# A macaron block: the prologue reordered so that the first feed-forward tile opens before all weights are examined

## The chip, the cores and the metric

One NeuronCore of a Trainium2 chip runs the whole program. The time is the device time of one execution in microseconds (us).

## The reference, cut to what matters

Input x has 8 x 1024 tokens of 256 features, all float32. Three residual steps follow each other:

```python
x = x + 0.5 * ffn(layernorm(x))      # ffn(r) = r + 0.5 * (silu(h(r) @ w1 + b1) @ w2 + b2)
x = x + mixer(layernorm(x))          # gated scan over time, 64 states, two projections
x = x + 0.5 * ffn(layernorm(x))
```

Here h(r) is a second layer norm with gamma and beta. The weights w1 (256 x 1024) and w2 (1024 x 256) come as int32 `q` with one scale for each group of 128 rows and each column: w = (q - 128) * scale. The products are made of `q - 128` alone and the scales are applied to the sums.

## The kernel before, in words

The 8192 tokens form 16 tiles of 512. Each stage (feed-forward, mixer, feed-forward) loops over the tiles; the whole input stays in SBUF (`resid`). Each engine has its own instruction list, written by hand, in which the work of neighbouring tiles is interleaved; semaphores join the lists. The slots of a feed-forward tile are f = 0 to 7, one for each block of 128 hidden features.

In slot f TensorE makes `half_products` (block f, first 128 features; two products of 128x512, for the rounded part `h_hi` and the remainder `h_lo`), one product pair `fc2` for each output half of block f - 4 (`LAG = 4`), and `add_products` (block f - 1, second 128 features). Between the two halves of fc1 the bank in PSUM is multiplied by `ratio` and gets `bias` (`scale_half`, on ScalarE, for f = 4 and 6 on VectorE). ScalarE then makes two silu (`g_full`, `g_hi`), GpSimd the remainder (`g_low`, L410), and VectorE adds each fc2 result to `z_acc` (`add_group`, L762). The layer norm of tile t + 2 (t + 1 in the prologue) is spread over the slots: `statistics` (L699) and `variance` on VectorE, `rsqrt` and most of `normalise` on GpSimd, the transposes (`turn`, L1002) on TensorE, `round_h` on ScalarE and `lower_h` (L745) on VectorE.

The kernel must also find out whether a weight is so large that its rounded form does not hold it exactly. `largest_of` reduces each quarter of `q` on VectorE as it lands (q1 in two pieces, q2 in two), `join_largest` joins the four, TensorE turns the column of maxima into a row, `find_width` reduces that and writes `wide_flag`. TensorE loads the flag (`value_load`) and branches to a program with one or with two parts for each weight. With these inputs the short one is taken.

Small vectors (scales, biases, gamma, beta and three mixer biases) are loaded as rows by 9 transfers of ScalarE's queue into `rows`, transposed once by TensorE and copied to `cols` by ScalarE. `beta_products` and `fold_beta` make the bias of fc1 out of beta, weights, scales and b1.

The order of the prologue on each engine before the change:

- ScalarE: 9 issues, silu table, `cols`, normalise blocks 2 and 3 of tile 0, `convert_q1(0)`, `round_h` twice, `convert_q1(1)`, all of q2, then the slots.
- VectorE: statistics and variance of tile 0, four `largest_of`, `join_largest`, reciprocal, `lower_h` c = 0, `find_width`, ratio, statistics and variance of tile 1, `fold_beta`, `lower_h` c = 1, a branch, then the slots; statistics and variance of tile 2 and half of tile 1's normalise in slot 3, statistics of tile 3 in slot 5, its variance in slot 7.
- GpSimd: constants, `rsqrt` of tile 0 (128x8: one column set for xhat, one for the residual), normalise blocks 0 and 1, `prepare_columns`, `residual` of tile 0, then the slots; `rsqrt` of tile 1 in slot 0.
- TensorE: transpose of rows, `turn` twice (after `cols_ready`), `beta_products(0)`, transpose of the maxima, `beta_products(1)`, branch, then slot 0 of tile 0. `turn` of tile 1 stands in slots 3 and 5.
- SyncE queue: x tile 0, q1, q2, x tiles 1 to 3, mixer weights and biases, x tiles 4 to 15.

Of the kernel before, what the change touches and what calls it, by code (L numbers as in the profile page):

```python
# [5 lines left out]
ALU = mybir.AluOpType  # L6
# [6 lines left out]
P = 128  # L13
# [8 lines left out]
def macaron_kernel(nc, x, wa, ba, wb, bb, wc, bc, wd, bd, wy, by, gamma, beta,  # L22
# [44 lines left out]
    R_AB = R_BETA + KC  # L67
    R_C = R_AB + 1
    ROWS = R_C + 1

    with ExitStack() as ctx:
# [15 lines left out]
        largest = sb("largest", [P, 6])  # L87
        wide_flag = sb("wide_flag", [1, 1], I32)
        beta_parts = sb("beta_parts", [P, KC, 2], F32R)
        beta_terms = sb("beta_terms", [P, FC, 2 * KC])  # L90
# [3 lines left out]
        ratio = sb("ratio", [P, FC])  # L94
# [9 lines left out]
        cols = sb("cols", [P, ROWS])  # L104
        ident = sb("ident", [P, P])
# [54 lines left out]
        rows_zero = sem("rows_zero")  # L160
# [9 lines left out]
        q2_ready = sem("q2_ready")  # L170
# [12 lines left out]
        wide_ready = sem("wide_ready")  # L183
# [9 lines left out]
        shift_ready = sem("shift_ready")  # L193
        xhat_ready = sem("xhat_ready")
# [96 lines left out]
        halves = (range(0, SUB // 2), range(SUB // 2, SUB))  # L291
        q2_halves = (slice(0, FC // 2), slice(FC // 2, FC))
# [21 lines left out]
        def _(sp):  # L314
# [43 lines left out]
        def _(pool):  # L358
            nc.gpsimd.memset(rows[:, :], 0.0).then_inc(rows_zero, 1)
# [9 lines left out]
            def rsqrt(ln, par, twice, shares=0):  # L369
# [11 lines left out]
                nc.gpsimd.tensor_tensor(shift[:, 0:n, :], rstd[:, 0:n, :], means, ALU.mult).then_inc(shift_ready, 1)  # L381

# [60 lines left out]
            def sum_bias():  # L443

                pool.wait_ge(mixer_loaded, 16 * 12)
# [21 lines left out]
            def feed_forward(ff0, ln0):  # L467
                def tile(t, par, before, behind):
                    ff, ln = t + ff0, t + ln0
                    residual_at, normalise_at = RESIDUAL_AT[before], NORMALISE_AT[before]  # L470
                    for f in range(FC):
                        if f >= 1:
                            g_low(ff, f - 1, par)
                        elif before:
                            g_low(ff - 1, FC - 1, 1 - par)
                        elif ff0 == 0:
                            rsqrt(ln0 + 1, 1, True)
                        if ff0 == 0 and not before and f == 1:
                            normalise(ln0 + 1, 1, 1, halves[0], True)
# [6 lines left out]
                        if behind >= 2 or ff0 == 0:  # L486
                            t2, twice = (t + 2, True) if behind >= 2 else (1 - behind, False)
                            if f == RSQRT_AT[before]:
# [32 lines left out]
        def _(act):  # L521
            act.wait_ge(rows_zero, 1)
# [8 lines left out]
            for v, r, at in ((ba, R_AB, 0), (bb, R_AB, N), (bc, R_C, N)):  # L531
                act.dma_start(rows[r:r + 1, at:at + N], v.rearrange("(a n) -> a n", a=1)).then_inc(rows_loaded, 16)
# [3 lines left out]

            act.wait_ge(rows_turned, 1)
            nc.scalar.activation(cols[:, :], ps_tr2[:, 0:ROWS], ACT.Copy).then_inc(cols_ready, 1)
            act.wait_ge(cols_ready, 1)
# [23 lines left out]
            def round_mixer(part):  # L563

                act.wait_ge(mixer_loaded, 16 * 12)
# [4 lines left out]
            def scale_half(ff, f):  # L570

                act.wait_ge(half_done, FC * ff + (f + 1))
                if type(ff) is int and ff == 0 and f == SCALED_ON_ACT[0]:
# [3 lines left out]
                                     scale=ratio[:, f:f + 1]).then_inc(scaled_on_act, 1)  # L577
# [33 lines left out]
            def feed_forward(ff0, ln0):  # L611
                def tile(t, par, before, behind):
                    ff, ln = t + ff0, t + ln0
                    for f in range(FC):
# [10 lines left out]
                        if f in TURN_OUT_AT[before]:  # L625
                            c = TURN_OUT_AT[before].index(f)
# [6 lines left out]
                        if (behind >= 2 or ff0 == 0) and f == 7:  # L633
# [3 lines left out]
                if ff0 == 0:  # L637
                    normalise(ln0, 0, 0, halves[1], xhat_half_ready)
                    convert_q1(0)
                    for c in range(KC):  # L640
                        round_h(ln0, ff0, 0, c, bank=(ps_tr, ps_tr2)[c])
                    convert_q1(1)
                    for k in range(KC):
                        act.wait_ge(q2_loaded[k], 16)
                    nc.scalar.activation(q2_sb[:, :, :], q2_int[:, :, :], ACT.Copy,
# [605 lines left out]
```

## Time and profile before

| what | value |
|---|---|
| median of 3 runs | 690.57 us (689.08 to 690.64) |
| profiled execution, its own time | 690.4 us |
| its span | 687.6 us |
| busy: TensorE, ScalarE, VectorE, GpSimd | 97%, 95%, 92%, 88% |
| mean granted TensorE clock | 0.999 |
| first product of 128x512 starts | 16.94 us |

The span runs from the first to the last instruction; the execution's own time is 2.8 us longer. All windows below are in us from the start of the span. The time of an instruction in a row includes its latency, so instructions of one engine that follow each other without a gap are closer together than their durations say.

### The profile page before, as it was taken

What the parts mean: (1) busy time and instruction counts of PE and PEld (TensorE: products, weight loads), DVE (VectorE), ACT (ScalarE), POOL (GpSimd) and SP (SyncE); (2) the same over time, 40 slices, a digit from 0 to 9 for tenths busy, and PEclk for the clock granted to TensorE, in tenths of its full rate; (3) what the DMA queues carried; (4) which work ended last, traced back from release to release, by engine and by line L of the source; (5) the groups of instructions that cost most, each with busy time, mean ns of one, the idle gap of its engine ahead of it and who ended that gap; (6) DMA issues with size and microseconds to landing.
All of it is one profiled execution on the core that took longest, in us unless ns stands there. A gap on an engine that the chain in (4) does not pass through costs nothing.

```text
span 687.6 us, 13669 instructions
## 1 busy us (share of the span) xinstructions
PE 668.0 (97%) x3224; PEld 539.2 (78%) x3224; DVE 634.8 (92%) x1329; ACT 653.4 (95%) x1095; POOL 604.8 (88%) x673
## 2 busy tenths in 40 slices
PE   3999999999999999999999999999999999999997
PEld 3678888888888878778877887788888888888885
DVE  5789999999999999889999998899999999999987
ACT  4899999999999999889999999999999999999994
POOL 4899999999999999857766789999999999999973
PEclk9999999999999999999999999999999999999999
DMA  8670000000000000000000000000000000000001
GB/s 254 172 236 4 1 0 0 0 0 0 0 0 0 1 0 2 1 1 1 0 0 0 0 1 1 30 33 32 31 31 31 31 31 31 31 31 32 32 32 63
DMA packets 19962, 20.22 MB, mean 29 GB/s; under 512 B 1564, under 2 KB 19666, under 8 KB 19922
## 3 DMA queue, kind: packets, MB, share of 16 engines
q1 hardware_dynamic: 19824, 19.74, 9.3%
q8 instruction: 16, 0.26, 0.2%
q14 instruction: 24, 0.20, 0.1%
q10 hardware_dynamic: 98, 0.02, 0.0%
HBM read 11.37 MB, written 8.39 MB: 29 GB/s over the span
## 4 chain that ended last, share of the span: by engine, by line
PE 90%; ACT 3%; DVE 3%; issue 2%; DMA 1%; ACTq 0%; POOL 0%; DVEq 0%; POOLq 0%
PE ps_z L1009 38%; PE ps_fc L1009 33%; PE ps_fc L1142 8%; PE ps_tr L1002 5%; PE ps_tr L1070 4%; PE ps_fc L1150 2%; PE ps_z L1002 1%; DMA rows<-in_L_attn_bc 1%; DVE z_acc L762 1%; ACT ps_fc L576 1%; ACT g_hi L593 1%; DVE stats L699 1%; ACT g_full L591 0%; DVE resid L887 0%; ACTq L530 0%
## 5 line engine op out<-in xcount | busy, mean ns | idle before, releaser
L410 POOL TENSOR_TENSOR g_lo<-g_full,g_hi 128x512 fp32r<-128x512 f32 x256 | 332.9, 1300 | 24.7 <-ACT g_hi L593 21.8
L762 DVE SCALAR_TENSOR_TENSOR z_acc<-ps_z,cols,z_acc 128x512 f32<-128x512 f32 (+1 forms) x449 | 322.2, 742 | 24.2 <-PE ps_z L1009 16.4
L1009 PE MATMUL ps_fc<-h_hi,q_sb 128*128 128x512 f32 x512 | 213.4, 417 | 1.4 <-ACT ps_fc L576 1.4
L1009 PE MATMUL ps_z<-g_hi,q_sb 128*128 128x512 f32 x512 | 202.4, 395 | 0.1
L1009 PE MATMUL ps_fc<-h_lo,q_sb 128*128 128x512 f32 x512 | 202.3, 395 | 0.0
L1009 PE MATMUL ps_z<-g_lo,q_sb 128*128 128x512 f32 x512 | 200.6, 392 | 0.0
L591 ACT ACTIVATE g_full<-ps_fc,safe_scale 128x512 f32<-128x512 f32 x256 | 194.8, 761 | 3.9 <-PE ps_fc L1009 2.2
L593 ACT ACTIVATE g_hi<-ps_fc,safe_scale 128x512 fp32r<-128x512 f32 x256 | 196.2, 766 | 0.0
L576 ACT ACTIVATE ps_fc<-ps_fc,bias,ratio 128x512 f32<-128x512 f32 x193 | 157.9, 819 | 1.8 <-DVE bias L873 1.8
L1009 PEld LDWEIGHTS ps_z<-g_hi,q_sb 128*128 128x128 f32 x512 | 96.1, 188 | 25.0 <-DVE z_acc L762 2.7
L1009 PEld LDWEIGHTS ps_fc<-h_hi,q_sb 128*128 128x128 f32 x512 | 97.3, 190 | 21.0 <-ACT ps_fc L576 2.1
L1009 PEld LDWEIGHTS ps_z<-g_lo,q_sb 128*128 128x128 f32 x512 | 96.1, 188 | 20.7
L1009 PEld LDWEIGHTS ps_fc<-h_lo,q_sb 128*128 128x128 f32 x512 | 97.6, 191 | 15.8
L375 POOL TENSOR_TENSOR rstd<-var_terms,minus_half 128x8 f32<-128x8 f32 (+1 forms) x48 | 70.7, 1472 | 11.7 <-DVE neg_mean L721 7.8
L400 POOL TENSOR_SCALAR resid<-resid,res_scale,shift 128x256 f32<-128x256 f32 x128 | 72.8, 570 | 0.2
L699 DVE BATCH_NORM_STATS2 stats<-resid 128x6 f32 (+1 forms) x192 | 69.2, 409 | 2.2 <-DMA resid<-in_L_attn_x 1.8
L583 ACT ACTIVATE z_acc<-ps_z,cols 128x512 f32<-128x512 f32 x64 | 58.0, 906 | 0.1
L389 POOL TENSOR_SCALAR xhat<-resid,rstd,shift 128x256 f32<-128x256 f32 x96 | 55.5, 579 | 0.2
L1142 PE MATMUL ps_fc<-wd_sb,q_int 128*128 128x256 f32 x240 | 54.6, 379 | 0.0
L739 DVE TENSOR_SCALAR ps_fc<-ps_fc,ratio,bias 128x512 f32<-128x512 f32 x63 | 50.9, 807 | 3.5 <-PE ps_fc L1009 3.5
L559 ACT ACTIVATE xhat<-resid,shift,rstd 128x256 f32 (+1 forms) x92 | 51.0, 602 | 0.0
L1002 PE MATMUL ps_tr<-ident,xhat 128*128 128x128 f32 x320 | 48.4, 274 | 2.1 <-ACT xhat L559 1.5
(110 smaller groups left out, 820.4 us busy)
## 6 DMA issues: line engine op xcount, KB each, us to landing
resid<-in_L_attn_x SPq DMA_DIRECT2D x15, 512.0 KB, 4.6
out_x<-resid SPq DMA_DIRECT2D x15, 512.0 KB, 2.9
q_int<-in_L_ffn_fc_q SPq DMA_DIRECT2D x4, 512.0 KB, 7.3
resid<-in_L_attn_x SPq DMA_DIRECT2D x2, 256.0 KB, 3.0
out_x<-resid SPq DMA_DIRECT2D x2, 256.0 KB, 2.7
wd_sb<-in_L_attn_Wd SPq DMA_DIRECT2D x1, 256.0 KB
wy_raw<-in_L_attn_Wy SPq DMA_DIRECT2D x2, 64.0 KB
bias_rows<-in_L_attn_by SPq DMA_DIRECT2D x1, 128.0 KB
```

Source lines behind the costliest of these rows:

```text
L375: nc.gpsimd.tensor_tensor(rstd[:, 0:n, :], var_terms[:, par, 0:n, :], minus_half[:, 0:n, :], ALU.pow).then_inc(rstd_ready, 1)
L400: last = nc.gpsimd.tensor_scalar(resid[:, t, a, :], resid[:, t, a, :], res_scale[:, a:a + 1], shift[:, 1, a:a + 1], ALU.mult, ALU.add)
L410: nc.gpsimd.tensor_tensor(g_lo[:, g % 4, :], g_full[:, g % 4, :], g_hi[:, g % 4, :].bitcast(F32), ALU.subtract).then_inc(g_ready, 1)
L576: nc.scalar.activation(bank, bank, ACT.Identity, bias=bias[:, f:f + 1], scale=ratio[:, f:f + 1]).then_inc(scaled_on_act, 1)
L583: nc.scalar.activation(z_acc[:, par, n, :], bank_of(0, n, par), ACT.Identity, bias=col(R_B2 + n), scale=col(R_S2 + n)).then_inc(z_begun[n], 1)
L591: nc.scalar.activation(g_full[:, g % 4, :], bank, ACT.Silu, scale=scale)
L593: nc.scalar.activation(g_hi[:, g % 4, :], bank, ACT.Silu, scale=scale).then_inc(g_hi_ready, 1)
L699: last = nc.vector.bn_stats(stats[:, a, :], resid[:, t, a, :])
L762: nc.vector.scalar_tensor_tensor(out=z, in0=bank_of(g, n, par)[:, tokens], scalar=col(R_S2 + KC * g + n), in1=z, op0=ALU.mult, op1=ALU.add ...
L1002: last = nc.tensor.transpose(bank[:, a * P:(a + 1) * P], xhat[:, par, a, c * P:(c + 1) * P], ident[:, :])
L1009: last = nc.tensor.matmul(out, w, v, start=start and i == 0, stop=stop and i == len(pairs) - 1, skip_group_check=not start)
L1142: nc.tensor.matmul(mix_bank(t, par, half)[:, a * D:(a + 1) * D], xn[:, par, k, at:at + P], wd_sb[:, k, :], start=False, stop=False, skip_g ...
```

## The change: what it does

1. **Small vectors.** The three mixer biases leave `rows` and go straight into a new tile `mixer_cols` by three transfers of SyncE's queue (64 elements each, one to a partition) ahead of the two `bias_rows` transfers. The memset of `rows` and ScalarE's wait for it go; ScalarE issues 6 transfers instead of 9.
2. **Tile 0's layer norm.** GpSimd makes only the xhat columns first (`rsqrt_first`, 128x4), and those of the residual (`rsqrt_rest`) after `prepare_columns`. ScalarE normalises before it copies `cols`. TensorE's `turn` no longer waits for `cols_ready`.
3. **q2.** ScalarE converts the first half, GpSimd the second, after tile 0's residual.
4. **Two flags.** The maxima of q1 alone give a first flag; those of q2 are taken after `fold_beta` and `lower_h` and give a second. TensorE opens tile 0 behind the first (`opening`: slots 0 to 3, with the second transpose of maxima inside it), then waits for the second flag and branches to the program, which begins tile 0 at slot 4.
5. **fold_beta.** `ratio` now also covers the second group of scales and `beta_terms` holds b1 times the reciprocal, so two of the five steps fall away.
6. **Tile 0's slots.** Tile 1's statistics stand behind the maxima of q2; its `rsqrt` moves to slot 2 of GpSimd, its normalise blocks 0 to 3 to slot 4 of VectorE, its `turn` to slots 5 and 7, `lower_h` to 6 and 7. Statistics of tile 2 go to slot 5 and its variance to 6; statistics and variance of tile 3 both to slot 7. ScalarE's share of tile 2's normalise moves from slot 7 of tile 0 to slot 0 of tile 1.

The core of the diff:

```diff
+        FIRST_TURN_AT, FIRST_LOWER_AT = (5, 7), (6, 7)
+        FIRST_RESIDUAL_AT = {5: (0, 1), 6: (2, 3)}
+        FIRST_NORMALISE_AT, FIRST_RSQRT_AT = {7: (0, 1, 2)}, 6
...
+            for v, at, i in ((ba, 0, 0), (bb, N, 0), (bc, N, 1)):
+                sp.dma_start(mixer_cols[at:at + N, i:i + 1], v.rearrange("(n a) -> n a", a=1)).then_inc(mixer_loaded, 16)
...
+            def rsqrt_first():
+
+                pool.wait_ge(terms_ready, 1)
+                nc.gpsimd.tensor_tensor(rstd[:, 0, :], var_terms[:, 0, 0, :], minus_half[:, 0, :],
+                                        ALU.pow).then_inc(rstd_ready, 1)
+                pool.wait_ge(rstd_ready, 1)
+                nc.gpsimd.tensor_tensor(shift[:, 0, :], rstd[:, 0, :], neg_mean[:, 0, :],
+                                        ALU.mult).then_inc(shift_ready, 1)
...
-                        elif ff0 == 0:
-                            rsqrt(ln0 + 1, 1, True)
-                        if ff0 == 0 and not before and f == 1:
-                            normalise(ln0 + 1, 1, 1, halves[0], True)
+                        if ff0 == 0 and not before and f == 2:
+                            rsqrt(ln0 + 1, 1, True, 1)
...
-                    rsqrt(ln0, 0, True)
+                    rsqrt_first()
                     normalise(ln0, 0, 0, halves[0], True)
                     prepare_columns()
+                    rsqrt_rest()
                     residual(ln0, 0, 1)
+                    pool.wait_ge(q2_loaded[1], 16)
+                    nc.gpsimd.tensor_scalar(q2_sb[:, q2_halves[1], :], q2_int[:, q2_halves[1], :], -ZERO_POINT, None,
+                                            ALU.add).then_inc(q2_ready[1], 1)
...
-                        if not before and f == 3:
+                        if ff0 == 0 and not before and f == LAG:
+                            normalise(ln0 + 1, 1, 1, halves[0], xhat_ready)
+                            normalise(ln0 + 1, 1, 1, halves[1])
+                        if ff0 == 0 and not before and f == 5:
+                            dve.wait_ge(x_loaded[0], 32)
+                            dve.wait_ge(aggr_done, ln0 + 2)
+                            statistics(2)
...
+                    join_largest(0, KC)
+                    prepare_ratios()
                     lower_h(ln0, ff0, 0, 0)
+                    find_width(0, KC + 2)
                     dve.wait_ge(beta_done, KC)
                     fold_beta(1)
                     lower_h(ln0, ff0, 0, 1, ps_tr2)
+                    for k, part in enumerate(q2_halves):
+                        largest_of(KC + k, q2_int[:, part, :].rearrange("p g d -> p (g d)"), q2_loaded[k])
+                    join_largest(1, 2 * KC + 2)
+                    dve.wait_ge(x_loaded[1], 16)
+                    dve.wait_ge(aggr_done, 1)
+                    statistics(1, halves[0])
+                    find_width(1, 2 * KC + 4)
+                    statistics(1, halves[1])
+                    variance(ln0 + 1, 1)
                     prepare_wide()
...
+            def opening(narrow):
+
+                for f in range(LAG):
+                    half_products(0, 0, f, 0)
+                    if narrow and f == LAG - 1:
+                        turn_all_largest()
+                    if f >= 1:
+                        add_products(0, 0, f - 1, 0)
+
+            def turn_all_largest():
+
+                pe.wait_ge(largest_found, 2 * KC + 3)
+                turn_largest(1)
...
-            pe.wait_ge(cols_ready, 1)
             for c in range(KC):
                 turn(0, 0, c, (ps_tr, ps_tr2)[c], 2, 1)
```

## Rows read from the trace of the kernel before

**Rows 1.** Page: the chain that ended last, shares by engine

```profile
PE 90%; ACT 3%; DVE 3%; issue 2%; DMA 1%; ACTq 0%; POOL 0%; DVEq 0%; POOLq 0%
```

**Rows 2.** Timeline of TensorE: start, duration, engine, line, out<-in, count, idle before

```profile
9.72 0.31 PE L994 MATMUL ps_z<-ident,rows 48*128 48x48 f32 x1 [9.72 <-DMA rows<-in_L_attn_bc]
11.55 1.09 PE L1002 MATMUL ps_tr<-ident,xhat 128*128 128x128 f32 x4 [1.52 <-ACT xhat L559]
...
13.14 1.85 PE L1055 MATMUL ps_z<-beta_parts,q_sb 128*128 128x2 f32 x8
...
15.21 1.87 PE L1055 MATMUL ps_z<-beta_parts,q_sb 128*128 128x2 f32 x8
16.94 0.77 PE L1009 MATMUL ps_fc<-h_hi,q_sb 128*128 128x512 f32 x1
...
19.64 0.76 PE L1009 MATMUL ps_fc<-h_hi,q_sb 128*128 128x512 f32 x1 [0.64 <-ACT ps_fc L576]
...
23.19 0.63 PE L1009 MATMUL ps_fc<-h_hi,q_sb 128*128 128x512 f32 x1
23.61 0.63 PE L1009 MATMUL ps_fc<-h_lo,q_sb 128*128 128x512 f32 x1
...
25.55 0.39 PE L1009 MATMUL ps_fc<-h_lo,q_sb 128*128 128x512 f32 x1
25.78 0.39 PE L1009 MATMUL ps_z<-g_hi,q_sb 128*128 128x512 f32 x1
...
36.88 0.50 PE L1009 MATMUL ps_z<-g_hi,q_sb 128*128 128x512 f32 x1
...
41.72 0.39 PE L1009 MATMUL ps_fc<-h_hi,q_sb 128*128 128x512 f32 x1
```

**Rows 3.** Timeline of VectorE

```profile
7.81 2.47 DVE L893 TENSOR_REDUCE largest<-q_int 128x1 f32<-128x1024 int32 x2 [1.93 <-DMA q_int<-in_L_ffn_fc_q]
...
15.26 0.28 DVE L905 TENSOR_REDUCE largest<-ps_z 1x1 f32<-1x128 f32 x1 [1.04 <-PE ps_z L1209]
...
19.72 1.41 DVE L699 BATCH_NORM_STATS2 stats<-resid 128x6 f32<-128x256 f32 x4 [0.41 <-issue]
...
21.80 0.73 DVE L729 TENSOR_SCALAR xhat<-resid,rstd,shift 128x256 f32<-128x256 f32 x2
25.98 0.82 DVE L739 TENSOR_SCALAR ps_fc<-ps_fc,ratio,bias 128x512 f32<-128x512 f32 x1 [3.46 <-PE ps_fc L1009]
...
33.20 0.73 DVE L745 SCALAR_TENSOR_TENSOR h_lo<-ps_tr,cols,h_hi 128x512 fp32r<-128x512 f32 x1
...
36.09 3.38 DVE L762 SCALAR_TENSOR_TENSOR z_acc<-ps_z,cols,z_acc 128x512 f32<-128x512 f32 x5
```

**Rows 4.** Timeline of ScalarE; ACTq is its sequencer issuing a transfer

```profile
3.94 0.27 ACTq L532 DMA_DIRECT2D rows<-in_L_attn_bc  x1
...
10.31 1.09 ACT L559 ACTIVATE xhat<-resid,shift,rstd 128x256 f32<-128x256 f32 x2
...
18.74 1.42 ACT L576 ACTIVATE ps_fc<-ps_fc,bias,ratio 128x512 f32<-128x512 f32 x2 [1.78 <-DVE bias L873]
```

**Rows 5.** Timeline of GpSimd

```profile
5.96 1.66 POOL L375 TENSOR_TENSOR rstd<-var_terms,minus_half 128x8 f32<-128x8 f32 x1 [3.62 <-DVE neg_mean L721]
...
22.21 1.47 POOL L410 TENSOR_TENSOR g_lo<-g_full,g_hi 128x512 fp32r<-128x512 f32 x1 [2.14 <-ACT g_hi L593]
```

**Rows 6.** Groups of GpSimd by form, whole span: busy us, mean ns | idle before

```profile
L410 POOL TENSOR_TENSOR g_lo<-g_full,g_hi 128x512 fp32r<-128x512 f32 x256 | 332.9, 1300 | 24.7 <-ACT g_hi L593 21.8 <-PE ps_z L1009 2.4
...
L400 POOL TENSOR_SCALAR resid<-resid,res_scale,shift 128x256 f32<-128x256 f32 x128 | 72.8, 570 | 0.2
...
L375 POOL TENSOR_TENSOR rstd<-var_terms,minus_half 128x4 f32<-128x4 f32 x16 | 17.6, 1097 | 3.6 <-POOL cs_parts L463 3.6
```

**Rows 7.** Timeline of SyncE's queue

```profile
19.27 0.56 SPq L335 DMA_DIRECT2D bias_raw<-in_L_attn_bd  x1
...
21.27 27.11 SPq L344 DMA_DIRECT2D resid<-in_L_attn_x  x12
```

More of the change, by code:

```diff
@@ L169, in macaron_kernel @@
         q1_ready = sem("q1_ready")
-        q2_ready = sem("q2_ready")
+        q2_ready = [sem(f"q2_ready{k}") for k in range(KC)]
         beta_ready = sem("beta_ready")
@@ L291, in macaron_kernel, with first_or @@
         halves = (range(0, SUB // 2), range(SUB // 2, SUB))
+        FIRST_TURN_AT, FIRST_LOWER_AT = (5, 7), (6, 7)
+        FIRST_RESIDUAL_AT = {5: (0, 1), 6: (2, 3)}
+        FIRST_NORMALISE_AT, FIRST_RSQRT_AT = {7: (0, 1, 2)}, 6
+        def first_or(ff0, before, first, usual):
+            return first if ff0 == 0 and not before else usual[before]
         q2_halves = (slice(0, FC // 2), slice(FC // 2, FC))
@@ L632, in tile @@
                             first_sum(ff, par, 1)
-                        if (behind >= 2 or ff0 == 0) and f == 7:
+                        if ff0 == 0 and before == 1 and f == 0:
+                            normalise(ln + 1, t + 1, 1 - par, REST, xhat_half_ready)
+                        if (behind >= 2 or ff0 == 0) and (ff0 or before) and f == 7:
                             normalise(ln + 2, t + 2 if behind >= 2 else 1 - behind, par, REST, xhat_half_ready)
@@ L787, in tile @@
                             add_group(ff if here else ff - 1, (f - LAG) % FC, par if here else 1 - par)
-                        if behind and f in H_LOWER_AT[before]:
-                            lower_h(ln + 1, ff + 1, 1 - par, H_LOWER_AT[before].index(f))
+                        lower_at = first_or(ff0, before, FIRST_LOWER_AT, H_LOWER_AT)
+                        if behind and f in lower_at:
+                            lower_h(ln + 1, ff + 1, 1 - par, lower_at.index(f))
                         if ff0 and not before and f == 0:
@@ L911, in prepare_wide, with lower_weights @@
+            def lower_weights(low, high, whole, full, count, ready):
+                nc.vector.tensor_scalar(whole.bitcast(F32), whole, -ZERO_POINT, None, ALU.add).then_inc(full, 1)
+                dve.wait_ge(full, count)
+                nc.vector.tensor_tensor(low, whole.bitcast(F32), high.bitcast(F32), ALU.subtract).then_inc(ready, 1)
             def prepare_wide():
-                dve.wait_ge(flag_ready, 1)
-                wide = dve.value_load(wide_flag[0:1, 0:1], min_val=0, max_val=1)
+                dve.wait_ge(flag_ready, 2)
+                wide = dve.value_load(wide_flag[0:1, 1:2], min_val=0, max_val=1)
@@ L1076, in tile @@
                     ff, ln = t + ff0, t + ln0
-                    for f in range(FC):
+                    for f in range(0 if before or ff0 else LAG, FC):
                         half_products(ff, ln, f, par)
@@ L1097, in tile @@
                             y_products(NT - 1, 1)
-                        if (behind or ff0 == 0) and f in TURN_AT[before]:
-                            c = TURN_AT[before].index(f)
+                        turn_at = first_or(ff0, before, FIRST_TURN_AT, TURN_AT)
+                        if (behind or ff0 == 0) and f in turn_at:
+                            c = turn_at.index(f)
                             if c and before:
@@ L1212, in _ @@
             pe.wait_ge(flag_ready, 1)
-            wide = pe.value_load(wide_flag[0:1, 0:1], min_val=0, max_val=1)
+            q1_wide = pe.value_load(wide_flag[0:1, 0:1], min_val=0, max_val=1)
+            with pe.If(q1_wide < 1):
+                q1_parts = (q1_sb,)
+                opening(True)
+            with pe.Else():
+                q1_parts = (q1_sb, q1_low)
+                turn_all_largest()
+                pe.wait_ge(q1_low_ready, KC)
+                pe.wait_ge(bias_ready, 1)
+                for k in range(KC):
+                    last = beta_products(k, q1_low)
+                last.then_inc(beta_low_done, 1)
+                pe.wait_ge(wide_bias_ready, 1)
+                opening(False)
+            pe.wait_ge(flag_ready, 2)
+            wide = pe.value_load(wide_flag[0:1, 1:2], min_val=0, max_val=1)
             with pe.If(wide < 1):
@@ L1218, in _ @@
                 q1_parts, q2_parts = (q1_sb, q1_low), (q2_sb, q2_low)
-                pe.wait_ge(wide_ready, KC + 1)
-                pe.wait_ge(bias_ready, 1)
-                for k in range(KC):
-                    last = beta_products(k, q1_low)
-                last.then_inc(beta_low_done, 1)
-                pe.wait_ge(wide_bias_ready, 1)
+                pe.wait_ge(q1_low_ready, KC)
+                pe.wait_ge(q2_low_ready, 1)
                 program()
```

176 lines of the change are left out of this document (86 added, 90 removed).

## The prediction

> **What bounds the kernel now.** I first read the chain of work that ended last: TensorE holds 90% of it [rows 1]. So nearly all of the span is TensorE's own work, and a prologue can only give back what lies ahead of TensorE's first unbroken stretch. Then I read TensorE's timeline. Nothing runs on it before the small vectors have landed at 9.72; `turn` of tile 0 starts at 11.55, the first product of fc1 at 16.94, then it waits 0.64 for the bias and runs on from 19.64 [rows 2]. In the first stretch the 512-column products stand 0.42 apart (23.19 to 23.61), from 25.55 on 0.23 apart: the lower and the upper level of its clock, 1.2 and 2.4 GHz [rows 2]. Slot 4 of tile 0 comes at about 25.2, slot 4 of tile 1 at 41.72 [rows 2]. The second date is my yardstick: from there on the order is the same in both kernels, each engine only waits for the others, and whatever is won or lost at 41.72 stays to the end.
>
> The timelines of the other engines say what these dates hang on. ScalarE normalises tile 0 only at 10.31, after `cols` [rows 4]. ScalarE's first scaling waits until 18.74 for the bias, which VectorE makes late because tile 1's statistics stand ahead of it [rows 4]. After its branch VectorE has a hole of 3.46 before 25.98 [rows 3]: it has made the statistics of tile 2 in front of it, at 19.72.
>
> **The change part by part: up to the first products.** Small vectors: three transfers fewer, so the last issue starts about 1.2 before 3.94 [rows 4] (three issues of some 0.3 and the wait for the memset). If the landing keeps its distance to the issue (9.7 - 3.9 = 5.7), it is at 8.5; if it goes by the count (9.7 x 6/9), at 6.5; if it is only the traffic of q1 and q2, still at 9.6. I take 7.5. What hides it is xhat: everything before 8.1 costs nothing.
>
> xhat of tile 0: the power on 128x8 took 1.66 from 5.96 [rows 5], on 128x4 it takes 1.10 [rows 6], and the 0.2 for `res_scale` falls away: shift ready at 7.3. ScalarE's two blocks (1.09, [rows 4]) end at 8.4, GpSimd's two as well. From the start of `turn` to the first product of fc1 TensorE needed 16.94 - 11.55 = 5.39, back to back [rows 2]; the same work now starts at 8.44 and ends at 13.8. Its inputs are there: `cols` follows on ScalarE at 8.4, q1's first conversion right behind it, as before; the q1 maxima are done at 10.3 (2.47 for the two from 7.81, [rows 3]). The branch on the first flag lies behind queued products, as before: nothing; if that cover is missing it costs its own length.
>
> The bias needs the last `beta_products` (13.8) and three small steps, 0.45: 14.4. The first half product is done at 13.8 + 0.85 + 0.2 = 14.9, one scaling takes 0.76 (1.42 for two, [rows 4]): the first `add_products` stands at 15.7 instead of 19.64. **TensorE's lead here: 3.9 us.**
>
> **From there to the yardstick.** Four pairs at 0.85 follow, then the transpose of all maxima at 19.1. VectorE has been ready for it: `lower_h` to 15.1, two maxima of q2 at 1.22 (2.47 for two, [rows 3]), the join, two blocks of statistics, 18.4. So it waits until 19.5, then `find_width` 0.4 (0.28 for its reduction, [rows 3]), two blocks of statistics 0.8, variance 0.7: 21.4. GpSimd's `rsqrt` of tile 1 (1.66 and two steps of 0.2, [rows 5]) ends at 23.5. In the kernel before it ended at about 20, since VectorE's normalise could start at 21.80 [rows 3]. TensorE is 3.9 early and tile 1's xhat 2 late.
>
> TensorE reaches slot 4 at 20.3. The second flag is there at 19.9. The branch is hidden: `turn` in slot 5 has to wait for xhat (24.9) anyway, some 0.9; a jump above about 1.5 us would count in full beyond that.
>
> Now VectorE has no hole left. Its list from 23.5 (each at its distance to the next: 0.66 for a 128x512 add, 3.38 for five, and for `lower_h`, 0.33 for a block of statistics, 0.70 for a scaling and for two blocks of normalise, [rows 3]): four blocks of normalise 1.40; two adds 1.32; statistics of tile 2 1.32; scaling 0.70; two adds 1.32; `lower_h` 0.66; variance 0.67; two adds 1.32; `lower_h` 0.66; statistics of tile 3 1.44; variance 0.67; the first add of group 4 0.75. Sum 12.2: it is done at 35.7. That add releases the bank for the second half of fc2's group 5, which before started at 36.88 [rows 2]. TensorE alone would have been there far earlier: 32 pairs at 0.456 and three `turn` of 0.36 are 15.7 from slot 4 to slot 4, so 36.0 at the yardstick, 4 us before VectorE lets it. **So most of the lead is spent on waiting: some 0.9 in slot 5, 0.9 in slot 7 for `lower_h`, 1.9 at about 33.8.**
>
> From 35.7 to slot 4 of tile 1 it is nine pairs and one `turn`, 9 x 0.456 + 0.36 = 4.46: 40.2, against 41.72. The same stretch took 4.84 before, 0.38 more than the sum [rows 2], for short waits on GpSimd; with those it is 40.6. The gain is 1.2 to 1.5; I take 1.2, since a sum of clean durations leaves such waits out everywhere.
>
> **What costs nothing and why.** q2's second half on GpSimd: no row has it; two inputs of 512 take 1.30, one of 256 takes 0.57 [rows 6], so 128x1024 lies between 2.0 (four times 0.5) and 2.6. GpSimd is free from 13.3 (residual of tile 0) to its first `g_low` at 17.9, and TensorE needs the half at slot 0 of tile 1; only above 4.5 would it delay anything. The three transfers of single elements on SyncE's queue: an issue took 0.56, so x tile 4 is asked for at 23 instead of 21.27 [rows 7]; it is read in tile 2, behind 41.72, and takes some 5 us. Without that cover it would be 1.7. Tile 3's x is issued ahead of them. ScalarE's normalise block in slot 0 of tile 1 is the same 0.5 as before in slot 7; GpSimd needs it only for tile 2's residual.
>
> VectorE and GpSimd side by side: the `g_low` that ran beside two blocks of VectorE's normalise took 1.47 [rows 5], the mean is 1.30 [rows 6]. Four blocks now stand beside `g_low` of groups 2 and 3: 0.3 on GpSimd, which TensorE doesn't see, as it waits for xhat there. The Trainium skill (GPSIMD Engine Reference, section Specifications) says that the two share their SBUF interfaces and get in each other's way when VectorE works in a two-port mode or with two SBUF inputs. The trace agrees by that row; if VectorE paid as well, the sum would be 0.3 worse.
>
> **The clock.** Before, the products went to the short spacing 5.6 us after the stretch from 19.64 began, in spite of products since 16.94 [rows 2]. Now the stretch begins at 15.7, so the rise is due near 21.3. Earlier gains little (VectorE binds); if it stayed at 25.2, slots 4 and 5 would take 6.8 instead of 3.7 and about 1.0 of the gain would go. The Trainium skill (TensorE: Matmul & The Clock Gate, Part 1) has the low clock as the resting state, which activity releases; the trace agrees, and it too puts the rise ahead of 25.2 here.
>
> **The rivals.** *The lead is kept.* If VectorE's list is shorter than I add it up, the 3.9 us stay: 690.4 - 3.9 = 686.5, or half of it, 688.4; [rows 1] and [rows 3] weigh against each other here. For it: TensorE is 90% of the chain. Against: VectorE was idle for 3.46 there before, and this is what the list fills. *Small vectors land as late as before* (9.6): `turn` at 9.9, everything 1.4 later, 690.6. For it: the DMA queues are full at that time. *The clock falls back* in the holes that the change makes (ends slower): TensorE stands still for 0.9, 0.9 and 1.9 us in 24 to 36. If the 1.9 drops it to the lower level, it takes another 5.6 us to rise: 13 products at 0.42 instead of 0.23, 2.6 us; 691.8. If it drops twice, 694.4; it is a slowdown that can be measured from 16 such products on. For it: with a gap of 0.64 before 19.64 the low level went on for 5 us. Against: that was before the rise, and the holes are short. *No effect*: chain unchanged is excluded, but all gains may be swallowed (jump of 3 us at the second flag): 690.6.
>
> **How the numbers follow.** The forecast: 0.60, 690.4 - 1.2 = 689.2 for an execution like the profiled one; the median of the runs is 0.17 above it, so 689.4. Lead kept wholly or by half: 0.15. Late landing or a long jump: 0.17. Clock: 0.08. About 0.3% (2.1 us) is what a measurement of this kernel can tell from no change. Faster by more: the lead kept, and a tail of the forecast, 0.18. Slower by more: half of the clock case and what I don't see, 0.07. Within: 0.75. The range: from 687.9 (two thirds of the lead kept) to 691.2 (late landing, 690.6 + 0.17, and a short wait more) leaves out about 0.2.
>
> **What would show it.** In the profile after: first `turn` at 8.4 to 8.8; first `add_products` near 15.7; spacing 0.23 from about 21; VectorE busy without a hole from 23.5 to 39; TensorE idle some 3.7 us between 20 and 36, released by VectorE; slot 4 of tile 1 at about 40.6; the rest of the span shifted as a whole. The prediction is wrong if TensorE has no idle time there, if the 0.42 spacing comes back after 25, or if later stages differ in length.

## The result: 698.8 us, 1.2% slower

| | median | runs | profiled execution, its span |
|---|---|---|---|
| before | 690.11 us | 689.08 to 690.64 | 690.4, 687.6 us |
| after | 698.76 us | 697.24 to 699.04 | 699.04, 697.2 us |

Each kernel ran four times beside the other, which is why the median of before differs a little from the one given further up. The ratio is 1.0122, with an interval of 1.0107 to 1.0137. The forecast was 689.4 with a range to 691.2 and a chance of 0.07 for slower: it was wrong in sign and by 9 us.

The page of the kernel after: span, busy time, and the shares of the chain that ended last.

```profile
span 697.2 us, 13683 instructions
...
PE 675.2 (97%) x3225; PEld 541.8 (78%) x3225; DVE 637.7 (91%) x1334; ACT 653.3 (94%) x1095; POOL 609.6 (87%) x673
...
PE 92%; DVE 3%; ACT 2%; issue 1%; POOL 1%; DMA 0%; DVEq 0%; ACTq 0%
```

The busy times of the kernel before, from its page:

```profile
PE 668.0 (97%) x3224; PEld 539.2 (78%) x3224; DVE 634.8 (92%) x1329; ACT 653.4 (95%) x1095; POOL 604.8 (88%) x673
```

TensorE is still the bound, and it has 7.2 us more busy time in a longer span. A lead or a delay of the prologue can't do that; something has made its work itself longer. The timeline of TensorE after (columns as in [rows 2]), from the first transpose to behind the yardstick:

```profile
7.33 0.31 PE L1037 MATMUL ps_fc<-ident,rows 46*128 46x46 f32 x1 [7.33 <-DMA rows<-in_L_ffn_ln_beta]
8.53 1.10 PE L1045 MATMUL ps_tr<-ident,xhat 128*128 128x128 f32 x4 [0.89 <-POOL xhat L418]
...
13.91 0.77 PE L1052 MATMUL ps_fc<-h_hi,q_sb 128*128 128x512 f32 x1 [0.20 <-issue]
...
16.04 0.77 PE L1052 MATMUL ps_fc<-h_hi,q_sb 128*128 128x512 f32 x1
...
18.66 0.39 PE L1052 MATMUL ps_fc<-h_hi,q_sb 128*128 128x512 f32 x1
...
28.39 0.77 PE L1045 MATMUL ps_tr<-ident,xhat 128*128 128x128 f32 x4 [3.63 <-DVE xhat L759]
28.80 0.78 PE L1052 MATMUL ps_fc<-h_hi,q_sb 128*128 128x512 f32 x1
...
31.08 0.63 PE L1052 MATMUL ps_fc<-h_lo,q_sb 128*128 128x512 f32 x1
31.51 0.63 PE L1052 MATMUL ps_z<-g_hi,q_sb 128*128 128x512 f32 x1
...
32.30 0.39 PE L1052 MATMUL ps_fc<-h_hi,q_sb 128*128 128x512 f32 x1
32.53 0.40 PE L1052 MATMUL ps_fc<-h_lo,q_sb 128*128 128x512 f32 x1
...
39.65 0.50 PE L1052 MATMUL ps_z<-g_hi,q_sb 128*128 128x512 f32 x1 [1.62 <-DVE z_acc L792]
...
44.41 0.39 PE L1052 MATMUL ps_fc<-h_hi,q_sb 128*128 128x512 f32 x1
```

Up to 16.04 the dates are the forecast's: `turn` at 8.53 (8.44), the first product at 13.91 (13.8), the first `add_products` at 16.04 (15.7) instead of 19.64 [rows 2]. Then TensorE stands still for 3.63 us, released by VectorE's xhat, and from there until 32.30 the products are 0.43 apart (31.08 to 31.51), the lower level of its clock. Slot 4 of tile 1, the yardstick, begins at 44.41, not at the forecast 40.6 nor at 41.72 as before. VectorE and GpSimd at that place:

```profile
19.44 0.28 DVE L945 TENSOR_REDUCE largest<-ps_z 1x1 f32<-1x128 f32 x1 [1.42 <-PE ps_z L1261]
...
21.00 0.74 DVE L745 TENSOR_SCALAR var_terms<-mean_var 128x4 f32<-128x4 f32 x1
...
24.12 4.21 DVE L759 TENSOR_SCALAR xhat<-resid,rstd,shift 128x256 f32<-128x256 f32 x4 [0.66 <-POOL shift L391]
28.25 1.40 DVE L792 SCALAR_TENSOR_TENSOR z_acc<-ps_z,cols,z_acc 128x512 f32<-128x512 f32 x2
```

```profile
13.41 2.79 POOL L530 TENSOR_SCALAR q_sb<-q_int 128x1024 fp32r<-128x1024 int32 x1
...
21.97 1.67 POOL L385 TENSOR_TENSOR rstd<-var_terms,minus_half 128x8 f32<-128x8 f32 x1 [0.24 <-DVE neg_mean L751]
...
24.05 3.81 POOL L439 TENSOR_TENSOR g_lo<-g_full,g_hi 128x512 fp32r<-128x512 f32 x3
```

The four blocks of `normalise` take 4.21 us on VectorE, where [rows 3] give 0.73 for two. They lie almost wholly beside three `g_low` of GpSimd, which take 3.81 us, 1.27 each, no more than elsewhere. GpSimd goes on undisturbed and VectorE pays: that is the first loss.

The second one is in the long stretches behind. The count of TensorE's products and transposes between 60 and 240 us, before and then after (windows; columns: busy us and count of PE, PEld, DVE, ACT, POOL, granted clock, DMA share, GB/s):

```profile
60.00:240.00 180.00, 180.00 (x878) 148.19 (x878) 173.82 (x352) 179.34 (x297) 174.41 (x198) 1.00 0.00 0
```

```profile
60.00:240.00 180.00, 180.00 (x865) 146.48 (x864) 170.64 (x347) 176.58 (x293) 172.46 (x195) 1.00 0.00 0
```

In both the engine is busy all the time and the granted clock is 1.00, yet after it gets through 13 fewer. All other engines do less as well: they follow. From 450 to 680 us it is 1101 instead of 1114; from 240 to 450 us, where the mixer lies, it is 1019 and 1020, so only the feed-forward stages lose. The timeline shows it product by product; before, then after, each from the start of an unbroken stretch to its end:

```profile
99.68 0.39 PE L1009 MATMUL ps_fc<-h_hi,q_sb 128*128 128x512 f32 x1
...
103.99 0.39 PE L1009 MATMUL ps_z<-g_lo,q_sb 128*128 128x512 f32 x1
```

```profile
101.59 0.40 PE L1052 MATMUL ps_fc<-h_lo,q_sb 128*128 128x512 f32 x1
...
104.16 0.39 PE L1052 MATMUL ps_fc<-h_hi,q_sb 128*128 128x512 f32 x1
```

Before, 19 steps in 4.31 us, 0.227 each; after, 11 steps in 2.57 us, 0.234 each, with the same duration of 0.39 in every row. From the start of one product to that of the next the mean is 0.2289 before and 0.2333 after, between 60 and 240 us; a tile of the feed-forward lasts 16.43 and 16.67 us. Over the some 30 tiles behind the yardstick that is 7.2 us, and the spans differ by 6.9 us beyond it (9.6 less the 2.7 at the yardstick); the tiles next to the mixer lose less than the others.

What can have changed there? Not the instructions. But the change resizes small tiles that are allocated ahead of the large ones (`largest`, `beta_terms`, `ratio`, `cols`, the new `mixer_cols`), and so every tile from `xhat` on (`h_hi`, `h_lo`, `g_hi`, `g_lo`, `z_acc`) lies 96 bytes further in each partition. The weights `q1_sb` and `q2_sb` are allocated ahead of them and stay. Before, h, g and the weights are all multiples of 256 bytes from each other; after, h and g are 96 bytes off. That became the main suspect.

### The profile page after: what moved, and what is told of

Same layout as the page of the kernel before. It is cut to its first block, busy times and chain, and to the rows that moved or that the text cites. A ratio compares the mean times of both kernels' runs of the same rounds, so it can differ in the third digit from the quotient of the medians.

```text
span 697.2 us, 13683 instructions
## 1 busy us (share of the span) xinstructions
PE 675.2 (97%) x3225; PEld 541.8 (78%) x3225; DVE 637.7 (91%) x1334; ACT 653.3 (94%) x1095; POOL 609.6 (87%) x673
## 4 chain that ended last, share of the span: by engine, by line
PE 92%; DVE 3%; ACT 2%; issue 1%; POOL 1%; DMA 0%; DVEq 0%; ACTq 0%
PE ps_z L1052 39%; PE ps_fc L1052 34%; PE ps_fc L1186 7%; PE ps_tr L1045 5%; PE ps_tr L1113 4%; PE ps_fc L1194 2%; PE ps_z L1045 1%; DVE stats L729 1%; DVE z_acc L792 1%; PE ps_z L1098 0%; DVE xhat L759 0%; DMA resid<-in_L_attn_x 0%; DVE resid L927 0%; DVE h_lo L775 0%; POOL h_lo L481 0%
## 5 line engine op out<-in xcount | busy, mean ns | idle before, releaser
L1052 PE MATMUL ps_z<-g_lo,q_sb 128*128 128x512 f32 x512 | 202.8, 396 | 0.0
L385 POOL TENSOR_TENSOR rstd<-var_terms,minus_half 128x8 f32<-128x8 f32 (+1 forms) x47 | 69.0, 1468 | 4.1 <-POOL cs_parts L492 3.9
L1045 PEld LDWEIGHTS ps_tr<-ident,xhat 128*128 128x128 f32 x320 | 40.0, 141 | 15.5 <-DVE xhat L759 4.1
```

The costliest lines, as they stand in the source:

```text
L385: nc.gpsimd.tensor_tensor(rstd[:, 0:n, :], var_terms[:, par, 0:n, :], minus_half[:, 0:n, :], ALU.pow).then_inc(rstd_ready, 1)
L1045: last = nc.tensor.transpose(bank[:, a * P:(a + 1) * P], xhat[:, par, a, c * P:(c + 1) * P], ident[:, :])
L1052: last = nc.tensor.matmul(out, w, v, start=start and i == 0, stop=stop and i == len(pairs) - 1, skip_group_check=not start)
```

## The experiments

All pads are tiles that nothing uses; [P, 8] is 32 bytes in each partition.

| run | what | h, g against the weights, mod 256 | us | ratio to before, interval |
|---|---|---|---|---|
| after | | 96 | 698.76 | 1.0122 (1.0107 to 1.0137) |
| e1 | after, pad 32 | 128 | 698.23 | 1.0127 (1.011 to 1.0144) |
| e2 | before, pad 32 | 32 | 695.57 | 1.0090 (1.0073 to 1.0107) |
| e3 | after, GpSimd waits | 96 | 696.73 | 1.0111 (1.0092 to 1.013) |
| e4 | e1 and e3 | 128 | 696.73 | 1.0113 (1.0096 to 1.013) |
| e5 | after, pad 416 | 0 | 692.72 | 1.0050 (1.0033 to 1.0067) |
| e6 | before, pad 512 | 0 | 689.91 | 1.0007 (0.9997 to 1.0016) |
| e7 | before, pad 128 | 128 | 695.12 | 1.0080 (1.0063 to 1.0097) |
| e8 | e5 and e3 | 0 | 690.42 | 1.0007 (0.9997 to 1.0016) |
| e9 | before, pad 256 | 0 | 689.67 | 0.9999 (0.9989 to 1.0008) |
| e10 | before, h alone by 128 | h 128, g 0 | 693.58 | 1.0048 (1.0032 to 1.0065) |
| e11 | before, g alone by 128 | h 0, g 128 | 693.37 | 1.0050 (1.0033 to 1.0066) |
| e12 | e5, layer norm earlier | 0 | 691.09 | 1.0017 (1.0007 to 1.0026) |
| e13 | before, all by 128 | 0 | 689.38 | 0.9999 (0.9989 to 1.0009) |
| e14 | before, weights alone by 128 | 128 | 695.91 | 1.0091 (1.0074 to 1.0107) |
| e15 | e8, statistics spread | 0 | 687.65 | 0.9977 (0.9968 to 0.9986) |
| e16 | e8, spread further | 0 | 690.23 | 1.0011 (1.0002 to 1.002) |

### The place of the tiles (e1, e2, e5, e6, e7, e9)

Each is one line ahead of `xhat`; of e2:

```diff
+        pad = sb("pad", [P, 8])
         xhat = sb("xhat", [P, 2, SUB, D])
```

> The changed kernel with one unused tile of 32 bytes a partition in front of xhat, so that xhat and every large tile behind it (h_hi, h_lo, g_full, g_hi, g_lo, z_acc) start at a multiple of 64 bytes again, as in the kernel before; in the changed kernel they start 32 bytes behind one. Nothing else differs. Theory A (the address sets the distance between products: 0.2333 us everywhere in the changed kernel, 0.228 in the mean before): feed-forward tiles last 16.43 us instead of 16.67, 30 tiles give back about 7 us, 698.8 becomes about 692. Rival B (the order of the prologue leaves the engines in another rhythm, addresses don't matter): within 0.5 us of 698.8. The four normalise blocks on VectorE (4.2 us) tell a third thing apart: if they are slow because xhat is no longer aligned they take 1.4 here, if it is GpSimd's work beside them they stay at 4.2.

> The kernel before with one unused tile of 32 bytes a partition in front of xhat: all large tiles from xhat on start 32 bytes behind a multiple of 64. Theory A: the products stand 0.2333 apart throughout, tiles of 16.67 us, about 690.1 + 7 = 697. Rival B: 690.1 within noise.

> The changed kernel with an unused tile of 416 bytes a partition in front of xhat. In the kernel before xhat and every large tile behind it start 128 bytes behind a multiple of 512, like resid and the weights; the run with 32 bytes only brought them to 256 behind one and gave back almost nothing. Theory A2: the distance of the products hangs on the place of the large tiles within 512 bytes (or on their distance to the weights), and 416 bytes bring back the one of before: feed-forward tiles of 16.43 us, about 698.8 - 6.5 = 692. Rival B2: the small tiles in front (ident, cols, ratio, bias), which moved too and stay moved here, or another difference of the program keep the products 0.2333 apart: 697 to 699.

> The kernel before with an unused tile of 512 bytes a partition in front of xhat: every large tile moves, but its place within 512 bytes stays. Theory A2: no change, 689.5 within noise. Rival: any move of these tiles, or only a distance beyond 512 bytes, makes the spacing 0.2333: 695 to 696, as the 32 bytes did.

> The kernel before with 128 bytes in front of xhat: all large tiles start at 256 behind a multiple of 512, as in the changed kernel with the 32-byte tile. If only the place within 64 bytes counts: 689.5. If the place within 512 counts (theory A2): 695 to 696.

> The kernel before with 256 bytes in front of xhat: the large tiles start at 384 behind a multiple of 512, thus at the same place within 256 bytes as before and at another within 512. If the place within 256 decides: 689.5. If it is the place within 512: 694 to 696.

32 unused bytes make the kernel before 6.0 us slower (e2), 128 make it 5.5 slower (e7), 256 and 512 change nothing (e9, e6). 416 on top of the change's own 96, which is 512 together, take 6.0 us off the kernel after (e5). So the place counts, and of the distances tried only multiples of 256 are free. e1 brought next to nothing: that missed its target, since 128 off is as bad as 96.

### Which tiles, and against what (e10, e11, e13, e14)

e10 moves `h_hi` and `h_lo`, e11 `g_hi` and `g_lo`, with a second pad that brings the rest back to a multiple of 512. e13 moves everything:

```diff
+        pad = sb("pad", [P, 32])
         resid = sb("resid", [P, NT, SUB, D])
```

e14 moves the weights, and what follows by 512 in all:

```diff
+        pad = sb("pad", [P, 32])
         q1_sb = sb("q1_sb", [P, KC, F], F32R)
...
+        pad2 = sb("pad2", [P, 96])
         xhat = sb("xhat", [P, 2, SUB, D])
```

> The kernel before in which only h_hi and h_lo are moved by 128 bytes within 512 (128 bytes in front of h_hi, 384 behind h_lo). If the place of the moving operand (the right-hand side that TensorE streams) makes the product slow: the products into ps_fc at 0.2333, those into ps_z as before, about half of the 5.5 us, 692. If it is the engines that write or read these tiles, or other tiles: 689.5.

> The kernel before in which only g_hi and g_lo are moved by 128 bytes within 512. By the theory of the moving operand: the products into ps_z slow, about 692. Otherwise 689.5.

> The kernel before with 128 unused bytes per partition in front of all tiles: resid, the weights, xhat, h, g and z_acc all move by 128 bytes, so their places against each other stay as they were. Theory 'relative' (what counts is where the tiles stand against each other, in pieces of 256 bytes): the time stays at 690, products 0.228 apart. Theory 'absolute' (128 behind a multiple of 256 is a good place, 0 a bad one): 695 or more, products 0.2333 apart.

> The kernel before with 128 unused bytes in front of the weights and 384 in front of xhat: the weights move by 128 bytes, xhat, h, g and z_acc by 512, which the earlier runs showed to cost nothing. Theory 'relative': as when h and g moved by 128 against the weights, 695. Theory 'absolute, of the streamed tiles': 690. Theory 'absolute, of all tiles': between, 691 to 693, since the weights alone would stand badly.

The same windows of e10, e13 and e14, a fence each:

```profile
60.00:240.00 180.00, 180.00 (x869) 147.17 (x868) 171.18 (x345) 177.56 (x295) 173.19 (x197) 1.00 0.00 0
```

```profile
60.00:240.00 180.00, 180.00 (x876) 148.04 (x876) 173.46 (x347) 178.92 (x298) 173.52 (x198) 1.00 0.00 0
```

```profile
60.00:240.00 180.00, 180.00 (x867) 146.81 (x866) 170.69 (x348) 176.63 (x294) 172.74 (x196) 1.00 0.00 0
```

All tiles moved together cost nothing (e13, 876 against 878), the weights moved alone cost 5.9 us (e14, 867) though h and g moved by 512, which alone costs nothing (e6). So it is the place of the streamed tile against the weights that counts, not the place by itself. The small tiles behind the weights moved with them in e14, but in e5 they stay where the change had put them, and the count there is 879. One of h and g moved costs 4.0 or 3.8 us (e10, e11), both 5.5 (e7): by the medians more than half each.

The loss is not spread evenly. With both operands 128 off (e7, e14), the mean step behind a product of `h_hi` or `g_hi` is 0.237 and behind one of `h_lo` or `g_lo` 0.2295, as before; at 96 off (the kernel after) all four are 0.233. In e10 it is 0.2328 behind `h_hi` and 0.2295 behind `g_hi`, but 0.2340 behind `g_lo`, which had not moved; in e11 `h_lo` is the slow one of the unmoved, 0.2339. Both stand just ahead of a product of the operand that moved. In the kernel before, a load of weights runs from 100.36 to 100.55 beside a product that streams from 100.13 to 100.52, and so with every product, so it is plausible that the two reads meet in SBUF by their distance. That is argued, not shown: in e10 neither the `g_lo` that streams nor the weights loaded beside it had moved, and that step is slow all the same. Why stays open.

### VectorE beside GpSimd (e3, e4, e8)

```diff
+                        if ff0 == 0 and not before and f == 3:
+                            pool.wait_ge(xhat_on_dve, 1)
```

It makes GpSimd's third `g_low` wait until VectorE has made xhat of tile 1, so that the two no longer overlap.

> The changed kernel in which GpSimd waits in slot 3 of tile 0 until VectorE has normalised tile 1, ahead of its g_low of group 2; the addresses stay as in the changed kernel. Theory C (VectorE's normalise is held up by GpSimd's instructions running beside it): the four blocks take 1.4 to 1.5 us instead of 4.2, TensorE's hole of 3.6 us shrinks to under 1, the products don't go back to the 0.43 spacing at 28.8, and slot 4 of tile 1 comes 3 to 4 us earlier than 44.4; 698.8 becomes about 695. Rival D (the blocks are slow because their data start 32 bytes behind a multiple of 64): they stay at 4.2, the time stays at 698.8 or gets worse by the delayed g_low.

> Both edits: the 32-byte tile and GpSimd's wait. Theories A and C together, if they add up: 698.8 - 7 - 3.5, about 688.3 to 689.4, a little under the kernel before, which is what the prediction had put down for the change. If they do not add up, the aligned tiles have no share in the prologue and it ends near 690.

> The changed kernel with GpSimd's wait for VectorE's normalise and the 416-byte tile. With GpSimd's wait the first transposes back of tile 0 came at 43.55, where the kernel before has 43.54. Theory A2: 689.5 within 0.7 us, equal to the kernel before. Rival B2: 696 to 697, as with the wait alone.

VectorE's four blocks, of e3 and then of e1, in which GpSimd doesn't wait:

```profile
24.11 1.38 DVE L761 TENSOR_SCALAR xhat<-resid,rstd,shift 128x256 f32<-128x256 f32 x4 [0.38 <-POOL shift L391]
```

```profile
24.05 3.28 DVE L760 TENSOR_SCALAR xhat<-resid,rstd,shift 128x256 f32<-128x256 f32 x4
```

1.38 us without GpSimd beside it, 3.28 with two `g_low` wholly beside it (e1), 4.21 with three (after). It is not the place of the data: e5, with its tiles back in place, has 4.21 as well. In the kernel after the first `g_low` had started just ahead of the blocks, at 24.05 against 24.12. A `g_low` that started while a block was already running took 1.47 before [rows 5] and 1.44 in e1. So it may hang on which of the two starts first who pays; no run tries that.

With the tiles in place the time went down by 2.3 us (e5 to e8, intervals apart). With the tiles out of place it is 2.0 by the medians (after to e3), but these intervals overlap, and half of e3's four executions had lost no clock (see below); at like granted clock e3 gains 0.9 to 1.5. Both repairs together are back at the time of before. From after to e5 and on to e8 it is 6.0 and 2.3 of the 8.7 us. The forecast gain of 1.2 is still missing.

### The layer norm earlier instead (e12)

e5 with tile 1's statistics and variance ahead of the second `find_width`, its `rsqrt` in slot 1 of GpSimd, and the wait one group earlier:

```diff
-                    statistics(1, halves[0])
+                    statistics(1)
+                    variance(ln0 + 1, 1)
                     find_width(1, 2 * KC + 4)
-                    statistics(1, halves[1])
-                    variance(ln0 + 1, 1)
```

> The changed kernel with the 416-byte tile, tile 1's statistics and variance in one piece ahead of find_width of the second flag, its rsqrt in slot 1 of GpSimd instead of 2, and GpSimd waiting for VectorE's normalise ahead of g_low of group 1 instead of 2. With the wait ahead of group 2 shift was ready at 24.1 and the time was 690.4. Now the terms are ready at about 19.4 instead of 21.9, rsqrt ends at 22.0, VectorE normalises from about 22.1: its list behind starts 2 us earlier, and if that list is what binds (the prediction's ledger) slot 4 of tile 1 and the end come 1 to 2 us earlier, 688.4 to 689.4. Rival: g_low of group 1 comes late (23.4 to 24.7 instead of 21.7), TensorE waits for it in slot 5, and nothing is gained: 690.4.

VectorE, then TensorE:

```profile
22.78 1.37 DVE L762 TENSOR_SCALAR xhat<-resid,rstd,shift 128x256 f32<-128x256 f32 x4
26.31 0.75 DVE L795 SCALAR_TENSOR_TENSOR z_acc<-ps_z,cols,z_acc 128x512 f32<-128x512 f32 x1 [2.16 <-PE ps_z L1054]
```

```profile
25.55 0.50 PE L1054 MATMUL ps_z<-g_hi,q_sb 128*128 128x512 f32 x1 [1.77 <-POOL g_lo L440]
```

xhat is there 1.3 us earlier, but now `g_low` is late: TensorE waits 1.77 for it, and VectorE, with nothing to add, loses 2.16. A second wait of 1.78 for VectorE stands at 37.77, where e8 has its own of 2.11. Part of the waiting has only changed its owner: 691.1, no better than e8. The profiled execution is one of the three fastest, 689.54.

### The missing gain: the clock (e15, e16)

In e8 TensorE has one longer wait, where VectorE's statistics and variance of tile 3 stand ahead of an add. TensorE, then VectorE, of e8:

```profile
36.95 0.50 PE L1055 MATMUL ps_z<-g_hi,q_sb 128*128 128x512 f32 x1 [2.11 <-DVE z_acc L795]
...
37.56 0.63 PE L1055 MATMUL ps_fc<-h_hi,q_sb 128*128 128x512 f32 x1
37.99 0.63 PE L1055 MATMUL ps_fc<-h_lo,q_sb 128*128 128x512 f32 x1
```

```profile
39.51 0.75 DVE L795 SCALAR_TENSOR_TENSOR z_acc<-ps_z,cols,z_acc 128x512 f32<-128x512 f32 x1 [0.64 <-PE ps_z L1055]
41.13 0.75 DVE L795 SCALAR_TENSOR_TENSOR z_acc<-ps_z,cols,z_acc 128x512 f32<-128x512 f32 x1 [0.87 <-PE ps_z L1055]
```

Behind the 2.11 us the products are 0.43 apart for 3.4 us, and VectorE, which had been the late one, now waits for them. e15 takes no work away, it spreads it:

```diff
-                            statistics(3)
-                        if not before and f == FC - 1:
+                            statistics(3, halves[0] if ff0 == 0 else range(SUB))
+                        if ff0 and not before and f == FC - 1:
+                            variance(ln0 + 3, 1)
+                        if ff0 == 0 and before == 1 and f == 0:
+                            statistics(3, halves[1])
+                        if ff0 == 0 and before == 1 and f == 1:
                             variance(ln0 + 3, 1)
```

e16 leaves one block in slot 7 and puts two in slot 0, one in slot 1 and the variance in slot 2.

> e8 (the change with the GpSimd wait and the tiles back in place) with two blocks of tile 3's statistics moved from slot 7 of tile 0 to slot 0 of tile 1 and its variance to slot 1. In e8 TensorE waited 2.11 us at 36.95 in one piece and then ran 8 products 0.42 apart, some 1.5 us more than at 0.23. Theory (the gain that is still missing went into the clock): the wait comes to about 0.8 (0.7 for two blocks and 0.7 for the variance less), the clock stays up, 688.9. Rival (VectorE's work is the bound, wherever it stands): the wait comes back in slots 0 and 1 of tile 1, 690.4 as before.

> As e15, but with one block of tile 3's statistics in slot 7 of tile 0, two in slot 0 and one in slot 1 of tile 1, the variance in slot 2. Theory (clock): the first wait about 0.5, no low spacing, 688.7, at most 0.3 better than e15. Rival (VectorE's work): 690.4.

TensorE in e15:

```profile
35.10 0.50 PE L1059 MATMUL ps_z<-g_hi,q_sb 128*128 128x512 f32 x1 [0.41 <-DVE z_acc L795]
35.44 0.40 PE L1059 MATMUL ps_z<-g_lo,q_sb 128*128 128x512 f32 x1
...
42.42 0.63 PE L1120 MATMUL ps_tr<-ident,z_acc 128*128 128x128 f32 x4
```

The wait is 0.41 (the longest of this prologue is now 1.08, at 25.45), the spacing stays at 0.23, and the first transpose of z_acc (`turn_back`) starts at 42.42; in the kernel before it was at 43.54, in e8 at 45.02. 687.65 us: 2.8 less than e8, and faster than both kernels, by 0.23% of before (0.14 to 0.32%). Theory and number agree in sign, and it gained 1.2 more than expected. The waits of VectorE between 39 and 44 us, 2.3 in e8, are gone too; that they are the 1.2 is not shown.

Single executions say the same, and their mean granted clock goes with them. Of ten of e8, nine took 689.99 to 690.51 at 0.995 to 0.997, and one 688.40 at 0.999; of ten of e12, three took 689.30 to 689.62 at 0.998 and 0.999, and seven 691.0 and more at 0.995 to 0.997. Of the four of e3, two took 695.8 at 0.998 and 1.0, and two 697.7 and 698.2 at 0.996. In the profiled executions of e1, e3 and e4 waits of 2.11, 2.06 and 2.09 were followed by products 0.23 apart. So with a wait of some 2 us the clock fell in most executions and not in all, at a price near 2 us. The executions of e15 lie between 687.48 and 688.93, all at 0.998 to 1.0. Of the 2.8 us from e8 to e15 the clock is thus some 2.0.

e16 is not understood. Its profiled execution was its fastest, 688.38, with 0.53 as the longest wait between 31 and 80 us and no stretch at the low spacing; the other ten took 689.84 to 691.52. The two slowest had a granted clock of 0.995 and 0.997, but the other eight had 0.998 to 1.0, as the fastest had: what made those 1.5 to 2.4 us slower was not the clock. The median is what the rival had said, 690.4. Why e15's split pays and e16's does not stays open.

## Why the prediction was wrong

- **"From there on the order is the same in both kernels ... whatever is won or lost at 41.72 stays to the end."** This step failed, and it is the larger part. The order was the same, the steps of TensorE were not: 0.2333 instead of 0.2289. The term was set at nothing; it measured 6.0 (e5 against after), and 5.5 to 6.0 on the kernel before with nothing else changed (e7, e2). The prediction named "if later stages differ in length" as what would prove it wrong (and "if the 0.42 spacing comes back after 25", which it did), but had no rival for it: I read the diff for instructions, not for sizes of tiles.
- **"Four blocks of normalise 1.40"** and "0.3 on GpSimd". Failed in size and in the engine that pays: 4.21 on VectorE, nothing on GpSimd. Both come from [rows 3] and [rows 5], where the overlap of the two was short. The Trainium skill (GPSIMD Engine Reference, section Specifications) says that the two share their SBUF interfaces, with contention when VectorE is in a two-port mode or has two SBUF inputs. The trace shows the contention, at 4.21 against 1.38 (e3); in which mode VectorE was, no run shows. The 0.3 by which I let it worsen the sum was far too little: it cost 2.3 in the end.
- **"Most of the lead is spent on waiting: some 0.9 ..., 0.9 ..., 1.9."** Right in kind and order, once the blocks take 1.4: in e8 the waits were 0.27, 0.57 and 2.11. In the kernel after the first one is 3.63.
- **The clock falls back** (0.08). This rival held: after the 3.63 in the kernel after, and after the 2.11 in e8. Its price of 2.6 for a wait of 1.9 was near the measured 2, though the clock came back after some 3.5 us and not after 5.6; its chance was much too low. Argued against it: "the holes are short". A gap of 2 us is not short.
- **The list of VectorE** bound, as argued: from 24.12 it has no gap but one of 0.17 until past 42. In e3 the second half of group 5 started at 36.93 against a forecast of 35.7 for this list; of the 1.2, 0.6 are GpSimd's `rsqrt`, done at 24.1 instead of 23.5 (ahead of it VectorE's `var_terms` had taken 0.74 in the kernel after, instead of 0.17), and most of the rest are steps in the list that took longer, such as `var_terms` at 0.57 and 0.47.
- **What held**: landing of the small vectors 7.33 (7.5), `turn`, first product, first `add_products`, transpose of the maxima 19.13 (19.1), `find_width` 19.44 (19.5). q2's half on GpSimd took 2.79, above my 2.6, and was hidden. The clock rose at 18.66, earlier than 21.3. One small slip of the sum: 41.72 less 40.6 is 1.1, not 1.2.
- **A term that I left out**: the part of an execution outside the span. It was 1.7 to 1.9 us in every profiled execution with the changed prologue and 2.5 to 2.8 in those with that of before. Over all executions of e15 and those of before beside them, the median span is 1.3 us shorter and the median part outside 0.6, which together make e15's 2.0 within the rounding. No run shows what makes that part shorter.

With the tiles in place, GpSimd kept away and the wait split, the rebuilt prologue is 1.1 us ahead at the first `turn_back` (42.42 against 43.54), of the 3.6 that it wins at 16.04. The change as it stood paid 6.0 for the places of its tiles, 2.3 for VectorE beside GpSimd, and some 2 for the clock. That the forecast of the gain comes out in e15, 1.3 in the span against 1.2, is in part luck: it took two repairs and a split of work that the prediction did not have.

## What to carry to other kernels

Compare the spacing of back-to-back products in a long stretch of both traces first: if it differs at the same granted clock, the cause is not in the schedule, and a resized small tile ahead of the large ones is enough; try the tiles that TensorE streams at a multiple of 256 bytes from its weights, as was best here. When an instruction of VectorE is moved, ask what GpSimd runs at that time and price the overlap by a row in which they overlap wholly. And see whether a wait of TensorE that can't be avoided can be split: 2.11 us in one piece cost some 2 us more in most executions, the 0.41 of e15 nothing. But measure each split, since e16 went further and lost the gain.

## What the runs showed of the hardware

- Products of 128x512 float32, each with a weight load of its own, stand 0.229 us apart on the mean when streamed tile and weights are a multiple of 256 bytes apart in their partition (before, e5, e6, e8, e9, e13), and 0.233 when they are 32, 96 or 128 off (e2, after, e7). 64 was not tried. The Trainium skill (TensorE: Matmul & The Clock Gate, Part 2, step-by-step) says that loading the next weights doesn't take read bandwidth of SBUF from the running product; e14 is hard to square with that, since moving the weights alone costs 5.9 us of 690. But what meets what was not isolated.
- A 128x256 VectorE operation with one SBUF source and two scalars per partition takes 0.35 us alone and up to 1.05 beside `g_low` on GpSimd (4.21 for four), and GpSimd's keeps its 1.27 there (after, e5).
- After some 2 us without work TensorE's clock fell to its lower level in some executions and not in others: the profiled one of e8 ran at it for 3.4 us behind a wait of 2.11, those of e1, e3 and e4 did not fall behind 2.11, 2.06 and 2.09. Within one kernel the mean granted clock and the time fall into two groups that go together (e8, e12), 1.6 to 2 us apart.
